# Two-layer graph kernel: VectorE instructions that take one of two tensor inputs from PSUM, a layer norm held in its PSUM bank, and tail gathers of 80 rows

## What is computed

```
# layer 0
x_t  = leaky(x @ W1n + b1n, 0.1) @ W2n + b2n            # per node, 64 -> 128 -> 64
e_t  = leaky(edge_attr @ W1e + b1e, 0.1) @ W2e + b2e    # per edge, 32 -> 64 -> 64
agg  = segment_sum(x_t[src] * e_t * dp_scale, dst)
g    = norm(x + agg * res_w) * gamma + beta
x    = norm(x + g)
# layer 1 (8 relations, 4 bases)
msg  = (sum_b w_comp[type, b] * x[src] @ weight[b]) * edge_weight
x    = norm(x + relu(segment_sum(msg, dst) + h_bias))
```

## Time and profile before

| | before |
|---|---|
| median of the runs, us | 4293.55 |
| profiled execution, span, us | 4331.8 |
| GpSimd (POOL) busy, us | 3276.1 |
| TensorE (PE) busy, us | 2734.1 |
| VectorE (DVE) busy, us | 2061.9 |
| ScalarE (ACT) busy, us | 513.8 |
| granted TensorE clock, share of full | 0.715 |

### The profile page before, as it was taken

The page is one execution under the profiler, slowest core; times in us unless marked ns, Lnnn a source line. Parts: engine busy times, 40 slices in busy tenths (PEclk is TensorE's granted clock), DMA queues, the critical chain, the costliest instruction groups (busy, mean ns, idle before and its releaser), DMA issues.

```text
span 4331.8 us, 58859 instructions
## 1 busy us (share of the span) xinstructions
PE 2734.1 (63%) x14343; PEld 2347.9 (54%) x14344; DVE 2061.9 (48%) x3776; ACT 513.8 (12%) x1256; POOL 3276.1 (76%) x3191
## 2 busy tenths in 40 slices
PE   7677776667666666667465555555555565555555
PEld 6555555555555555555455555555555555555555
DVE  5333334343444444454554555555455555555555
ACT  3111112222212222222100000000000000000000
POOL 3777777777777777777677777777777777777776
PEclk9766667776777777777666767767677666677767
DMA  3222222222222222222111111111111111111111
GB/s 83 42 39 38 39 41 42 39 40 39 40 44 41 41 43 41 41 43 41 27 26 24 26 25 25 27 25 27 24 27 27 25 27 26 26 27 27 28 25 27
DMA packets 506007, 147.48 MB, mean 34 GB/s; under 512 B 403200, under 2 KB 455540, under 8 KB 505978
## 3 DMA queue, kind: packets, MB, share of 16 engines
q0 software_dynamic: 100096, 102.70, 12.5%
q1 hardware_dynamic: 405882, 44.44, 7.4%
HBM read 137.28 MB, written 9.62 MB: 34 GB/s over the span
## 4 chain that ended last, share of the span: by engine, by line
POOL 69%; issue 22%; PE 3%; DVE 2%; POOLq 1%; ACT 1%; DVEq 1%; DMA 1%; SPq 0%; ACTq 0%
POOL rows L494 69%; PE ps_o L1015 1%; PE ps_agg L1083 1%; PE ps_o L1074 1%; POOLq L487 0%; PE ps_z L1062 0%; POOLq L491 0%; DMA rows<-node_table,src_ix 0%; PE ps_z L1007 0%; PE ps_x L1007 0%; PE ps_fin L1126 0%; DVEq L721 0%; DVE hid L803 0%; POOLq L505 0%; DVE work L867 0%
## 5 line engine op out<-in xcount | busy, mean ns | idle before, releaser
L494 POOL DMA_INDIRECT rows<-node_table,src_ix x3128 | 3254.7, 1041 | 983.5 <-issue 951.8
L1089 PE MATMUL ps_agg<-work 128*128 128x128 f32 x6256 | 1197.3, 370 | 899.1 <-DVE work L954 898.1
L1089 PEld LDWEIGHTS ps_agg<-work 128*128 128x128 f32 x6256 | 1106.4, 275 | 988.7 <-DVE work L954 986.9
L954 DVE TENSOR_TENSOR work<-rows,attr 128x1024 f32<-128x1024 f32 x391 | 483.5, 1237 | 830.5 <-DMA rows<-node_table,src_ix 830.1
L754 DVE TENSOR_TENSOR work<-iota_f,rel 128x512 f32<-128x512 f32 x782 | 542.1, 693 | 349.7 <-DVE acc L768 235.9
L1083 PE MATMUL ps_agg<-work 128*64 128x128 f32 x3128 | 598.3, 354 | 13.6 <-issue 12.8
L1083 PEld LDWEIGHTS ps_agg<-work 128*64 128x64 f32 x3128 | 476.5, 182 | 109.4 <-issue 107.3
L1070 PE MATMUL ps_o<-b2e,ones 3*128 3x256 bf16 x391 | 125.8, 322 | 596.2 <-DVE hid L803 595.6
L810 DVE TENSOR_TENSOR work<-ps_o,rows 128x256 f32<-128x256 f32 x391 | 165.3, 423 | 637.8 <-DMA rows<-node_table,src_ix 634.5
L1070 PEld LDWEIGHTS ps_o<-b2e,ones 3*128 3x128 bf16 x391 | 36.7, 94 | 713.9 <-DVE hid L803 704.2
L1074 PE MATMUL ps_o<-W2e_d,hid 128*128 128x128 f32 x1564 | 360.6, 367 | 0.0
(11 more groups left out here) (101 smaller groups left out, 1055.3 us busy)
## 6 DMA issues: line engine op xcount, KB each, us to landing
rows<-node_table,src_ix POOLq DMA_INDIRECT x3128, 2.4
attr<-in_edge_attr_dram SPq DMA_DIRECT2D x78, 320.0 KB
node_table<-x_sb SPq DMA_DIRECT2D x14, 224.0 KB
node_table<-work SPq DMA_DIRECT2D x24, 128.0 KB, 2.0
out_dram<-x_sb SPq DMA_DIRECT2D x13, 224.0 KB
src_ix<-in_src_dram SPq DMA_DIRECT2D x156, 10.0 KB, 2.0
dst_ix<-in_dst_dram SPq DMA_DIRECT2D x156, 10.0 KB
attr<-in_edge_type_dram SPq DMA_DIRECT2D x78, 10.0 KB, 2.2
```

The source lines that it names most:

```text
L494: nc.gpsimd.indirect_dma_start(rows[:, slot_of(u), j, :], None, table, bass.IndirectOffsetOnAxis(ap=src_ix[:, half_of(u), col : col + 1], ...
L954: nc.vector.tensor_tensor(scaled[:, ring, :, :, :], rows[:, slot_of(u), :, :].rearrange("p j (o f) -> p j o f", o=1).to_broadcast([P, J, B ...
L1089: last = nc.tensor.matmul(bank[:, pr * P : (pr + 1) * P], scaled[:, ring, j, 2 * pr : 2 * pr + 2, :].rearrange("p b f -> p (b f)"), hot[:, ...
```

## The change

Seven edits:

1. `iota_f` is copied once into the upper half of the bank `ps_x` (`iota_ps`), and `one_hot` and the type comparison read it there. `rel` stays in SBUF.
2. `coef` moves from SBUF into the bank `ps_z`; `scale_rows` reads it there.
3. `is_rel` moves from SBUF into the bank `ps_o[0]`.
4. `centred` moves from SBUF into `ps_fin`, the very columns that TensorE wrote, so that `finish0` and `finish1` write over what they read.
5. `layer_norm` writes the difference from the mean into a new SBUF tile `deviation` (where `centred` was), squares that, and takes the reciprocal of the deviation into `inv_std`, seven columns of `ps_fin`, which the last multiplication reads.
6. `fin_read` is raised at the end of `finish0` and `finish1`.
7. The four gathers of the tail tile of each layer take 80 rows.

```
+        iota_ps = ps_x[:, 2 * P : 3 * P]
+        coef = ps_z[:, 0 : 2 * GJ * B].rearrange("p (h e b) -> p h e b", h=2, b=B)
+        is_rel = ps_o[0][:, 0 : GJ * R].rearrange("p (e r) -> p e r", r=R)
+        centred = ps_fin[:, 0 : CH * F].rearrange("p (b f) -> p b f", f=F)
+        inv_std = ps_fin[:, CH * F : CH * F + CH]
...
-                        rows[:, slot_of(u), j, :], None, table,
-                        bass.IndirectOffsetOnAxis(ap=src_ix[:, half_of(u), col : col + 1], axis=0),
+                        rows[0:n, slot_of(u), j, :], None, table,
+                        bass.IndirectOffsetOnAxis(ap=src_ix[0:n, half_of(u), col : col + 1], axis=0),
...
-                gather(l, BODIES, 0, FULL + 1 - BODY)
+                gather(l, BODIES, 0, FULL + 1 - BODY, n=TAIL_P)
...
+            nc.vector.tensor_copy(iota_ps, iota_f[:])
...
-                    iota_f[:].rearrange("p (o n) -> p o n", o=1).to_broadcast([P, J, P]),
+                    iota_ps.rearrange("p (o n) -> p o n", o=1).to_broadcast([P, J, P]),
...
-                link_c(nc.vector.tensor_tensor(centred, centred, over_features(mean), ALU.subtract))
-                link_c(nc.vector.tensor_tensor(squares, centred, centred, ALU.mult))
+                link_c(nc.vector.tensor_tensor(deviation, centred, over_features(mean), ALU.subtract))
+                link_c(nc.vector.tensor_tensor(squares, deviation, deviation, ALU.mult))
...
-                link_c(nc.vector.reciprocal(var, var))
-                return nc.vector.tensor_tensor(target, centred, over_features(var), ALU.mult)
+                link_c(nc.vector.reciprocal(inv_std, var))
+                return nc.vector.tensor_tensor(target, deviation, over_features(inv_std), ALU.mult)
...
-                dve.sem_inc(fin_read[0], 1)
                 link_c(layer_norm(link_c, c * 2 + 1, centred))
...
                 link_c(layer_norm(link_c, c * 2 + 2, x_c))
+                dve.sem_inc(fin_read[0], 1)
                 dve.sem_inc(normed[0], 1)
```

More of the change, by code:

```diff
@@ L118, in bass_gnn_resnorm_d2_kernel @@
         at_w = 2 * J * B * F
-        is_rel = work[:, at_w : at_w + GROUP * J * R].rearrange("p (e r) -> p e r", r=R)
-        at_w += GROUP * J * R
         coef_terms = work[:, at_w : at_w + GROUP * J * B * R].rearrange("p (e b r) -> p e b r", b=B, r=R)
@@ L126, in bass_gnn_resnorm_d2_kernel @@
         at_w += 2 * J * P
-        centred, squares = (
+        deviation, squares = (
             work[:, at_w + k * CH * F : at_w + (k + 1) * CH * F].rearrange("p (b f) -> p b f", f=F) for k in range(2)
@@ L143, in bass_gnn_resnorm_d2_kernel @@
         enorm = attr_flat[:, 2 * GJ : 4 * GJ].rearrange("p (h e) -> p h e", h=2)
-        coef = attr_flat[:, 4 * GJ : (4 + 2 * B) * GJ].rearrange("p (h e b) -> p h e b", h=2, b=B)
         rel = sb("rel", [P, 2, GROUP, J])
@@ L481, in _, with gather @@
             stage(PAIRS - 1, 0)
-            def gather(l, i, u, slot_used=None):
+            def gather(l, i, u, slot_used=None, n=P):
                 table = (node_table, node_table2)[l]
@@ L897, in finish1 @@
                     centred, ps_fin[:, 0 : CH * F].rearrange("p (b f) -> p b f", f=F), over_blocks(hbias_r[:]), ALU.add))
-                dve.sem_inc(fin_read[1], 1)
                 x_c = x_sb[:, bass.ds(c * CH, CH), :]
@@ L901, in finish1 @@
                 link_c(layer_norm(link_c, c + (2 * CHUNKS + 1), x_c))
+                dve.sem_inc(fin_read[1], 1)
                 dve.sem_inc(normed[1], 1)
@@ L928, in coefficients @@
                     etype[:, h, :].rearrange("p (e o) -> p e o", o=1).to_broadcast([P, GROUP * J, R]),
-                    iota_f[:, 0:R].rearrange("p (o r) -> p o r", o=1).to_broadcast([P, GROUP * J, R]),
+                    iota_ps[:, 0:R].rearrange("p (o r) -> p o r", o=1).to_broadcast([P, GROUP * J, R]),
                     ALU.is_equal))
```

## The result

The changed kernel takes 4037.72 us (median of 4 runs, 4037.32 to 4041.27), the kernel before on the same chip 4289.83 (4 runs, 4283.32 to 4296.34). The ratio is 0.9417, interval 0.9402 to 0.9432: 252 us or 5.8% less. The forecast was 4000 with 3970 to 4055.

A forecast was written before the change was run, and what follows sets the result against it. GpSimd's 3128 gathers, each duration plus 0.305 us, were taken as the bound. Span 4331.8 - 301.9 + 6 - 1.4 gave 4034.5 us; allowing for timed runs below the profiled execution, the forecast was 4000 us, range 3970 to 4055.

The forecast's parts named there:

- The bound and its cause: GpSimd's gathers set the pace; VectorE instructions with two SBUF inputs stretch them by 301.9 us over 944 ns each.
- The sum on the span: Profiled span: 4331.8 us less 301.9, plus 6 for the square, less 1.4 for tail gathers, gives 4034.5 us.
- Left under the square: Layer norm's square keeps two SBUF inputs; 39 instances beside gathers leave 6 us of stretch.
- The tail's gathers: Eight gathers of 80 rows instead of 128 save 0.18 us each, 1.4 us in all, ends 0 and 2.8.
- the fixed phases: Outside the gathers: 80.8 us to the first start, about 22 between layers, 21 after the last.
- from the span to the timed runs: Profiled execution 38.3 us above timed median: 3996 us if an offset, 4035 if timed runs have less stretch; chose 4000.
- VectorE's time: A PSUM input costs VectorE the same; PSUM output taken as 0; 3.0 us per layer 1 tile, off the path.
- fin_read: Raised later, at the layer norm's end: cost 0, without cover up to 12 us for each chunk.
- what is late next: Gathers come each 4.996 us per tile; TensorE at 4.44 and 3.78 and VectorE at 3.0 stay below; GpSimd remains the bound.
- Part: Rival: scale_rows (L954) holds gathers by rows read or what it writes; gain 134 us, time 4160; chance 0.04.
- nothing: Rival: the stretch follows VectorE's activity, operands' place no matter; time 4293 us; chance 0.03.
- VectorE as the bound through slow PSUM operands: Rival: broadcast operands from PSUM run slower, over 2.2 times as long; at 2.4 times 4405 us; chance 0.01.

The follow-up runs named there:

- the pair of added comparisons: Changed kernel plus an unread comparison behind each one-hot: iota from SBUF 4133.42 us (ratio 0.9497), iota from PSUM 4051.13 us (0.9308).
- the two single edits: Kernel before with only the one-hot's iota in PSUM, 4275.43 us (ratio 0.9825), or only coef in PSUM, 4158.30 us (0.9554).
- both with is_rel: Kernel before with iota, coef and is_rel in PSUM, layer norm in SBUF, tail gathers of 128 rows: 4049.04 us, ratio 0.9301.
- second trace: Kernel before, unchanged, profiled again in a later job: span 4358.7 us; its timed runs 4348.13 us, ratio 0.9991.
- first comparison: Changed kernel against the kernel before, chip not recorded: 4037.72 against 4289.83 us, ratio 0.9417.
- chip C: Slow chip of the last four runs; changed kernel 6385.55 us against kernel before 6108.10 (ratio 1.0451), in a later job 6265.79 against 5931.58 (1.0594).
- its two near variants: Changed kernel with the square as deviation times centred in PSUM, 4035.41 us; iota, coef and is_rel in PSUM with the layer norm in SBUF, 4049.04 us.

## Why the prediction was right, and where it was not

*The bound and its cause.* Right. The stretch by two SBUF inputs was 301.9 us and is 2.2; the pair of added comparisons shows the operand's place alone to be worth 82 us, and the two single edits bring 81 and 198 us, 279 together, where both with is_rel bring 307 on the same chip. The edit of is_rel was not run alone; in the kernel before, some 16 us of stretch lay under its instructions, so the parts do not simply add up.

*The sum on the span.* 4034.5 against 4035.5, which is luck in part: three terms are off and nearly cancel. Left under the square: 6 expected, 3.1 measured. I took a gather to be held for all the time to the instruction's end, and it is held 0.12 us less, and not at all when it starts in the first 0.05 us; 39 x (0.625 - 0.17)^2 / 2 / 1.249 = 3.2. The gathers as a whole kept 2.2 us over 944 each, where 6 - 1.4 = 4.6 was my sum. The tail's gathers take about 0.90 us, not 0.77: 48 rows fewer save 0.04 to 0.05 us, 0.4 us in all and not 1.4. And the fixed phases were taken as unchanged and are not: between the layers 24.7 us and not 22.05, after the last gather 22.5 and not 21.5. They are not fixed in the kernel before either: its second trace has 23.7 and 21.9. The last tile's one-hot of layer 0, in the kernel before and in the changed one:

```profile
2085.81 0.69 DVE L754 TENSOR_TENSOR work<-iota_f,rel 128x512 f32<-128x512 f32 x1
```

```profile
2037.89 0.69 DVE L759 TENSOR_TENSOR work<-ps_x,rel 128x512 f32<-128x512 f32 x1
```

The last gather ended at 2084.94 and at 2034.42, so VectorE was 0.9 us behind it and is now 3.5. In the second trace of the kernel before it was 1.95. That VectorE catches up more slowly after a chunk, when a tile's gathers come each 4.996 us, would explain the rest; no run separates the two. I had asked only whether it catches up in the middle.

*The step that failed: from the span to the timed runs.* I put 4000 because three runs within 13 us looked to me "more like an offset than like another pattern of stretches". The runs speak for the pattern. Where both are known, the time is the span plus 1.8 us; by that the kernel before's first profiled execution took 4333.6 us, 44 more than the median of the runs around it. Its own time was not recorded, so this is inferred, but the second trace shows what can differ: 26.2 of the 26.9 us between the two spans are stretch. The other of my two readings, 4035, was the right one. So the gain in the timed runs is 252 us and not 297, and what was mis-sized is the stretch of the timed runs, 301.9 in my sum: 4289.8 - 1.8 less the 4030 us that the earlier trace rows give without stretch (80.8 + 3128 x 1.249 + 22 + 21) is 257.

*VectorE's time, fin_read, what is late next.* Right in the first comparison's trace: a PSUM input costs nothing, GpSimd never waits for a message over 0.3 us, and no turn of a chunk came late: TensorE's waits before L1131 and L1166 are within 1 us of those before L1126 and L1161 in all. On chip C GpSimd does wait, so that it is the bound is a premise that belongs to the chip too.

*The rivals.* Part and nothing: refuted by the coef edit and the pair. The part's own price was off too: it gave L954 163 us of layer 1's stretch, and the trace before has 190.8 under it. VectorE as the bound through slow PSUM operands: refuted by 1218 ns for scale_rows, where more than 2.2 times 1237 was needed. Slower did occur, on one chip, by a way that I had not listed.

## What to carry to other kernels

Where GpSimd's indirect DMAs set the pace, look at their durations and not only at the gaps: a median far below the maximum says that something holds them. Then look for VectorE instructions with two SBUF tensors or fast SBUF copies; one input in PSUM cost VectorE nothing here and freed GpSimd. When one profiled execution and the timed runs differ by a per cent, price the change from both, and time it on more than one chip.

## What the runs showed of the hardware

- A gather that starts over 0.05 us behind the start of a VectorE instruction with two SBUF inputs, and over 0.12 us before its end, ends 0.82 us behind that end (611 of 611 well inside these limits, kernel before); one that starts earlier or later isn't touched. With one input in PSUM none of 348 was.
- The four-byte SBUF-to-SBUF copy of 512 elements takes 0.417 us in the median, and 782 of them add 17.5 us of stretch. It holds gathers at two places, and a gather holds it: copies that start 0.52 to 0.77 us behind a gather's start end 1.19 us behind it (114 of 120).
- An indirect DMA of 128 rows of 256 bytes takes 0.944 us of GpSimd, one of 80 rows about 0.90, and the next follows 0.305 us later. Nearly all of it is fixed: 48 rows fewer save 0.04 us.
- Off chip C, the changed kernel repeats within 4 us and its two near variants within 3.2; the kernel before spread over 13, 45 and 41 us in its three jobs, and from 4283 to 4375 over all of them.
- Chip C ran all kernels 1.4 to 1.6 times as long, with gathers of the usual duration, and their DMA packets took no longer.
